# Mixture-of-experts tail of a four-batch attention kernel: 15 whole tiles at the end, or 16 steps of two half tiles in two runs that begin while the last batch is still being routed

## What is computed

```python
x = x + L0_xattn(layernorm(x), ctx, mask0)          # 2 heads of 64, context 512
x = x + L0_ffn(layernorm(x))                        # sigmoid(xr@Wr) * (relu(xk@Wk)**2 @ Wv), xk/xr mix a token with the one before it
x = x + L1_xattn(layernorm(x), ctx, ctx, mask1)     # 16 heads of 8, context 512
h = layernorm(x)
e = argmax(h @ router.T)                            # 8 experts, one for each token
x = x + down[e] @ (silu(gate[e] @ h) * (up[e] @ h)) # gate, up: 352x128; down: 128x352
```

## Time and profile before

| | us |
|---|---|
| median of 3 runs | 301.01 |
| lowest and highest | 298.39, 303.46 |
| the profiled execution, its own time | 302.52 |
| its span, first to last instruction | 300.7 |
| mean granted clock of TensorE | 0.92 of full |

### The profile page before, as it was taken

One profiled execution on the slowest core, in us unless ns is written; L12 is line 12 of the kernel. 1 busy time (PEld: TensorE's weight loads), 2 busy tenths in 40 slices (PEclk: granted clock), 3 DMA queues, 4 the chain that ended last, 5 costly groups with the idle time before them and its releaser, 6 DMA issues.

```text
span 300.7 us, 5435 instructions
## 1 busy us (share of the span) xinstructions
PE 254.9 (85%) x1878; PEld 135.1 (45%) x1878; DVE 186.5 (62%) x637; ACT 142.5 (47%) x268; POOL 75.3 (25%) x90
## 2 busy tenths in 40 slices
PE   0799998695898999999999999999998421999993
PEld 0345666464453244444434343343434220477872
DVE  3280966869877676778768868678643251244551
ACT  1167464433044366546666655656666100244540
POOL 2643592605203400003110203002031211023443
PEclk9999999899596699999999999999999855599997
DMA  6990366240646349998001940042000003601000
GB/s 180 401 416 11 99 152 157 59 134 25 148 117 163 101 149 275 289 256 259 13 2 34 291 203 2 0 147 83 2 0 2 35 0 109 192 8 33 18 16 2
DMA packets 19083, 34.46 MB, mean 115 GB/s; under 512 B 1407, under 2 KB 16386, under 8 KB 18096
## 3 DMA queue, kind: packets, MB, share of 16 engines
q1 hardware_dynamic: 9408, 23.58, 25.6%
q10 hardware_dynamic: 8784, 8.95, 11.3%
q0 software_dynamic: 864, 1.58, 1.6%
HBM read 21.74 MB, written 12.82 MB: 115 GB/s over the span
## 4 chain that ended last, share of the span: by engine, by line
PE 48%; DVE 9%; ACT 6%; issue 3%; DMA 2%; POOL 1%; POOLq 0%; DVEq 0%; SPq 0%; ACTq 0%
PE banks L1186 9%; PE banks L1172 8%; PE banks L1102 7%; PE banks L1167 5%; DVE scores_unused L839 5%; PE banks L1241 4%; PE banks L1242 3%; ACT p_region L626 3%; PE banks L1263 3%; PE banks L971 2%; ACT q_region L610 2%; PE banks L1255 2%; PE banks L977 1%; DMA binned_dram<-token_rows,mask_bias 1%; PE banks L1072 1%
## 5 line engine op out<-in xcount | busy, mean ns | idle before, releaser
L839 DVE CUSTOM_DVE_ANT_0 scores_unused<-banks,mask_bias 128x512 bf16<-128x512 f32 x128 | 82.8, 688 | 22.8 <-PE banks L1102 22.0
L626 ACT ACTIVATE p_region<-banks 128x1024 f32<-128x1024 f32 x64 | 65.3, 1022 | 57.4 <-PE banks L1172 57.2
L1102 PE MATMUL banks<-k_region,q_region 80*128 80x512 bf16 x128 | 41.9, 401 | 2.1 <-DVE max L839 1.7
L426 POOL TENSOR_TENSOR ln_rstd<-ln_var_eps,minus_half 128x2 f32<-128x2 f32 x16 | 12.2, 764 | 123.6 <-DVE ln_var_eps L692 123.6
L1172 PE MATMUL banks<-q_region,k_region 80*128 80x256 bf16 x256 | 40.3, 282 | 0.0
L1186 PE MATMUL banks<-p_region,values 128*9 128x256 f32 x512 | 34.3, 388 | 1.0 <-ACT p_region L626 1.0
L1172 PEld LDWEIGHTS banks<-q_region,k_region 80*128 80x128 bf16 x256 | 20.2, 99 | 16.8 <-issue 15.0
L1167 PE MATMUL banks<-mask_bias_by_key,ident_bf 64*64 64x512 bf16 x256 | 26.8, 408 | 0.6 <-ACT q_region L610 0.6
L515 POOL DMA_INDIRECT out_dram<-q_region x15 | 14.7, 979 | 34.0 <-DVE q_region L960 33.0
L950 DVE SCALAR_TENSOR_TENSOR q_region<-q_region,banks 128x352 f32<-128x352 f32 x15 | 7.8, 522 | 24.0 <-ACT q_region L655 24.0
L509 POOL DMA_INDIRECT binned_dram<-token_rows,mask_bias x8 | 8.3, 1038 | 55.4 <-DVE mask_bias L822 54.1
(11 more groups left out here) (146 smaller groups left out, 399.5 us busy)
## 6 DMA issues: line engine op xcount, KB each, us to landing
binned_dram<-ctx_region ACTq DMA_DIRECT2D x1, 8224.0 KB, 37.0
k_region<-k_parts_dram SPq DMA_DIRECT2D x4, 1152.0 KB
k_region<-gate_up_dram SPq DMA_DIRECT2D x1, 2816.0 KB, 13.2
q_region<-q_parts_dram SPq DMA_DIRECT2D x12, 192.0 KB
k_region<-mask1k_dram SPq DMA_DIRECT2D x1, 2048.0 KB, 12.0
k_region<-mask_dram SPq DMA_DIRECT2D x1, 2048.0 KB, 16.4
q_region<-binned_dram SPq DMA_DIRECT2D x15, 128.5 KB, 2.7
k_parts_dram<-q_region SPq DMA_DIRECT2D x4, 384.0 KB, 2.8
```

Of the source, the lines that this page charges most:

```text
L626: a.activation(pt[:, u % 2, j, :, :].rearrange("p (c t) q -> p c (t q)", c=2), ps[:, c:c + 2, :], ACT.Exp, scale=float(D1) ** -0.5).then_i ...
L839: return v.tensor_tensor_reduce(out=junk[:, q, :], in0=scores, in1=m1b[:, QT * (u // 4) + q, :], scale=1.0, scalar=-3e38, op0=ALU.add, op1 ...
L1102: return m.matmul(out, qst[0:R, (u * GH + j) * SQ + q * P:(u * GH + j) * SQ + (q + 1) * P], kst[0:R, (u * GH + j) * SK:(u * GH + j + 1) * ...
```

## The change

1. **Two runs.** Batches 0 to 2 (768 tokens) and batch 3 (256 tokens) have bins and tables of their own. The first run has 10 steps, the second 6: 16 in one pipeline.
2. **Half tiles.** A step still takes 128 rows, but as two halves of 64, each with its own expert and place (20 and 12 halves are enough for any split). Every product with expert weights is issued twice, once for each half, to PSUM partitions 0 to 63 and 64 to 127.
3. **Weights of the second half.** The first half reads its expert in the resident weights `moe_w` at a register's address. The second half's expert (1088 floats on 128 partitions, 557 KB) is copied from DRAM for each step by SyncE into a ring `stage` of seven places. The rows of a step come with two DMAs of 64 rows.
4. **Registers.** TensorE loads the one register it needs at the start of each step (`load_expert`), 16 times, in place of 15 at once. SyncE loads its own in seven loads.
5. **Batch 3 between the steps.** `BEHIND` is gone; `BESIDE2` puts `oT` to `pos`, `cnt` and `tab` (the table) of batch 3 between the parts of steps -1 to 4. Batch 2's chain moves up by a slot or so, and `cnt` and `tab` of the first run stand at (14, 3) and (15, 0).

```diff
-SLOT_TILES = (TOK - E) // P + E
+HALF = P // 2
+PHASE_BATCHES = (range(B - 1), range(B - 1, B))
+PHASE_TOK = tuple(SQ * len(bs) for bs in PHASE_BATCHES)
+PHASE_STEPS = tuple((E + (n - E) // HALF + 1) // 2 for n in PHASE_TOK)
+PHASE_AT = (0, PHASE_STEPS[0])
+STEPS = sum(PHASE_STEPS)
...
+EXPERT = 2 * I + 3 * D
+STAGES = 7
+STAGES_SOONER = 3
...
-    (13, 1): [("oT", 2)], (13, 2): [("wO", 2)], (14, 0): [("s4", 2)], (14, 1): [("n4", 2)], (14, 2): [("nT", 2)],
-    (14, 3): [("lg", 2), ("hot", 2)], (15, 1): [("pos", 2)],
+    (13, 1): [("oT", 2)], (13, 2): [("wO", 2)], (13, 3): [("s4", 2)], (14, 0): [("n4", 2)], (14, 1): [("nT", 2)],
+    (14, 2): [("lg", 2), ("hot", 2)], (14, 3): [("cnt", 0)], (15, 0): [("pos", 2), ("tab", 0)],
 }
-BEHIND = [(name, B - 1) for name in ("oT", "wO", "s4", "n4", "nT", "lg", "hot", "pos")] + [("cnt", 0)]
+BESIDE2 = {(-1, 1): [("oT", 3)], (0, 0): [("wO", 3), ("s4", 3)], (1, 0): [("n4", 3)], (1, 1): [("nT", 3)], (2, 0): [("lg", 3)],
+           (2, 1): [("hot", 3)], (3, 1): [("pos", 3), ("cnt", 1)], (4, 1): [("tab", 1)]}
...
+            def weights_in(s):
+
+                if s >= STAGES:
+                    sp.wait_ge(y_ready, s - STAGES + 1)
+                sp.dma_start(stage[:, s % STAGES, :], moe_d[:, bass.ds(second[s] * EXPERT, EXPERT)]).then_inc(staged[s % STAGES], 16)
...
             sp.wait_ge(experts_done, 1)
...
+            where(0, range(0, 2))
+            whose(0, range(0, STAGES_SOONER))
+            for s in range(STAGES_SOONER):
+                weights_in(s)
+            sp.wait_ge(scattered, 16 * QT * len(PHASE_BATCHES[0]))
+            for s in range(0, 2):
+                rows_in(0, s)
+            where(0, range(2, PHASE_STEPS[0]))
+            for s in range(2, PHASE_STEPS[0]):
+                rows_in(0, s)
+            whose(0, range(STAGES_SOONER, PHASE_STEPS[0]))
+            sp.wait_ge(st_ready, UNITS * GH)
+            for s in range(STAGES_SOONER, PHASE_STEPS[0]):
+                weights_in(s)
+            sp.wait_ge(experts_done, 2)
+            first = PHASE_AT[1]
+            where(1, range(first, first + 2))
+            whose(1, range(first, first + 2))
             sp.wait_ge(scattered, 16 * TILES)
...
-            pe.wait_ge(experts_done, 1)
-            _, expert = nc.values_load_multi_w_load_instructions(experts, engines=[pe.engine], min_val=0, max_val=E - 1,
...
+            def load_expert(s):
...
+                pe.wait_ge(experts_done, ph + 1)
+                n = s - PHASE_AT[ph]
+                _, r = nc.values_load_multi_w_load_instructions(experts[ph][:, n:n + 1], engines=[pe.engine], min_val=0, max_val=E - 1,
...
+            def half_weights(s, r, c, n):
+
+                if r == 0:
+                    return moe_w[:, bass.ds(expert[s] * EXPERT + c, n)]
+                return stage[:, s % STAGES, c:c + n]
...
                 if there(s + 1):
-                    e = expert[s + 1]
+                    load_expert(s + 1)
                     pe.wait_ge(gT_copied, s + 2)
+                    pe.wait_ge(staged[(s + 1) % STAGES], 16 * ((s + 1) // STAGES + 1))
                     if s >= 1:
                         pe.wait_ge(h_done, s)
-                    m.matmul(ps[:, 2 + 2 * nxt, 0:I], ginT[:, nxt, :], gu[:, bass.ds(e * (2 * I), I)], start=True, stop=True)
-                    m.matmul(ps[:, 3 + 2 * nxt, 0:I], ginT[:, nxt, :], gu[:, bass.ds(e * (2 * I) + I, I)], start=True, stop=True)\
-                        .then_inc(gu_ready, 1)
+                    for k in range(2):
+                        first, second = (half_weights(s + 1, r, k * I, I) for r in range(2))
+                        m.matmul(ps[0:HALF, 2 + k + 2 * nxt, 0:I], ginT[:, nxt, 0:HALF], first, start=True, stop=True)
+                        last = m.matmul(ps[HALF:P, 2 + k + 2 * nxt, 0:I], ginT[:, nxt, HALF:P], second, start=True, stop=True)
+                    last.then_inc(gu_ready, 1)
...
-                    for n, (c, rows) in enumerate(ITILES):
-                        last = m.matmul(ps[:, 6, 0:P], hT[0:rows, nxt, n * P:(n + 1) * P], dn[0:rows, n, bass.ds(e * D, D)],
-                                        start=n == 0, stop=n == 2)
+                    for n, (_, rows) in enumerate(ITILES):
+                        first, second = (half_weights(s - 1, r, 2 * I + n * D, D) for r in range(2))
+                        c = n * P + HALF
+                        m.matmul(ps[0:HALF, 6, 0:P], hT[0:rows, nxt, c - HALF:c], first[0:rows], start=n == 0, stop=n == 2)
+                        last = m.matmul(ps[HALF:P, 6, 0:P], hT[0:rows, nxt, c:c + HALF], second[0:rows], start=n == 0, stop=n == 2)
```

More of the change, by code:

```diff
@@ L329, in pipeline @@
         def pipeline(step):
-            for s in range(-2, SLOT_TILES + 1):
-                step(s, s % 2, lambda n: 0 <= n < SLOT_TILES)
+            for s in range(-2, STEPS + 1):
+                step(s, s % 2, lambda n: 0 <= n < STEPS)
         @block.sync
@@ L411, in _, with where @@
-            sp.wait_ge(scattered, 16 * TILES)
-            for s in range(SLOT_TILES):
-                sp.dma_start(gin[:, s, :], bins_d[bass.ds(at[s] * P, P), :]).then_inc(gin_in[s], 16)
+            sp.dma_start(moe_w[:, 7 * EXPERT:], moe_d[:, 7 * EXPERT:]).then_inc(moe_w_in, 16)
+            at, second = {}, {}
+            def where(ph, steps):
+                n = len(steps)
+                lo = 2 * (steps[0] - PHASE_AT[ph])
+                _, r = nc.values_load_multi_w_load_instructions(row_halves[ph][:, lo:lo + 2 * n], engines=[sp.engine], min_val=0,
+                                                                max_val=E * BIN_HALVES[ph] - 1,
+                                                                skip_runtime_bounds_check_because="the table is clamped to it")
+                for k, s in enumerate(steps):
+                    at[s] = r[2 * k:2 * k + 2]
@@ new lines, in whose @@
+            def whose(ph, steps):
+                lo = PHASE_STEPS[ph] + steps[0] - PHASE_AT[ph]
+                _, r = nc.values_load_multi_w_load_instructions(experts[ph][:, lo:lo + len(steps)], engines=[sp.engine], min_val=0,
+                                                                max_val=E - 1,
+                                                                skip_runtime_bounds_check_because="the table is clamped to it")
+                for k, s in enumerate(steps):
+                    second[s] = r[k]
@@ new lines, in _ @@
+            for s in range(STAGES_SOONER, PHASE_STEPS[0]):
[4 more added lines that the diff above has]
+            whose(1, range(first, first + 2))
+            sp.wait_ge(scattered, 16 * TILES)
+            for s in range(first, first + 2):
+                rows_in(1, s)
+                weights_in(s)
+            where(1, range(first + 2, STEPS))
+            for s in range(first + 2, STEPS):
+                rows_in(1, s)
@@ L414, in _ @@
+            whose(1, range(first + 2, STEPS))
+            for s in range(first + 2, STEPS):
+                weights_in(s)
             for r in range(YBUFS):
-                sp.wait_ge(out_done[r], 16 * len(range(r, SLOT_TILES, YBUFS)))
+                sp.wait_ge(out_done[r], 16 * len(range(r, STEPS, YBUFS)))
         @block.gpsimd
@@ L499, in _, with scatter @@
             output_bias(3)
-            pool.wait_ge(ids_set, 1)
-            for b in range(B):
-                inverse_root("s4", b)
-                if b == 0:
-                    pool.wait_ge(bins_blank, 16)
+            def scatter(b):
                 pool.wait_ge(ln4_done, b + 1)
@@ L643, in _ @@
             copy_out(UNITS - 1)
-            for kind, b in BEHIND:
-                beside(kind, b)
-            act.wait_ge(slot_done, B)
             def step(s, par, there):
@@ L660, in step @@
                     a.activation(ginT[:, par, :], ps[:, 0, 0:P], ACT.Copy).then_inc(gT_copied, 1)
+                for kind, b in BESIDE2.get((s, 0), []):
+                    beside(kind, b)
                 if there(s):
@@ L668, in step @@
                     last.then_inc(hT_copied, 1)
+                for kind, b in BESIDE2.get((s, 1), []):
+                    beside(kind, b)
             pipeline(step)
@@ L793, in beside @@
                     places(b)
+                if kind == "cnt":
+                    halves_of_experts(b)
+                if kind == "tab":
+                    table(b)
             def per_tile(c, b):
```

182 lines of the change are left out of this document (111 added, 71 removed).

## The result

| | before | after |
|---|---|---|
| median, same series (us) | 301.35 (4 runs) | 322.67 (4 runs) |
| lowest and highest | 298.39, 303.46 | 317.98, 325.88 |
| profiled execution: time, span | 302.52, 300.7 | 325.88, 324.0 |
| its mean granted clock | 0.92 | 0.908 |
| start of the last unit's transposes (`oT`) | 235.50 | 250.60 |

The ratio is 1.066 (95% interval 1.043 to 1.088). The forecast was 302, with 293 to 317 as its range: too low by some 21 us, outside the range, and a slower kernel where "within 2%" was the likeliest.

A forecast was written before the change was run, and what follows sets the result against it. TensorE's 18.4 us pause after the attention and its 2.29 us steps bound the kernel. 14.6 us won at the start, less 4.0 (ramp), 2.3 (extra step), 7.4 (12 steps), 2.0 (batch 3, tail): 302, range 293 to 317.

The forecast's parts named there:

- Costs at nothing: ScalarE ... stay below TensorE: In the expert steps, ScalarE's 1.13 us and GpSimd's 0.87 us a step stay below TensorE's step and cost nothing.
- The floor by the weights of gate 3: Gate 3's weights, issued behind 20 row loads and two register loads, land at 252.4; it doesn't decide gate 3 at 254.5.
- the ramp: From the first row transpose at 239.7 to gate 3 at 254.5: 10.8 us as now plus 4.0 us, at the lower clock.
- Its last weights ... land by 281, before gate 13: Batch 3's last weights, six copies with eight row loads behind the first four, land by 281, before gate 13.
- The clock back at 1.2 GHz in the pauses of the steps: TensorE's clock falls in pauses between steps, making it slow; 0.03 chance, together with weights or rows later than their cover.
- the term that decides: TensorE's one-register load each step, between down and gate: 0.5 us long, adding 0.38 us a step, ends 0 and 1.87.
- the halves run beside each other: In gate, up and down, both half products overlap: no doubling counted, 0 for down, which was the less sure.
- The changes of shape: Each step goes from full-width transposes to half products and back: 2 x 0.12 = 0.24 us a step.
- the load is hidden: Rival: the register load costs nothing, the step is 2.53 us and the time 296.3; chance 0.28.
- The staged weights bind: Rival: steps wait for their 557 KB at 218 GB/s and rows, some 3.0 us a step, 303, inside the forecast.
- The load stalls: Rival: the register load between down and gate stalls TensorE a microsecond or more a step, 312 to 322; chance 0.24.
- the halves of down don't overlap: Rival: the two half products of down run one after the other, 13 x 0.64 = 8 us, 310; chance 0.05.

## Why the prediction was wrong, point by point

1. **The step that failed: "Costs at nothing: ScalarE ... stay below TensorE".** It counted ScalarE's work in the steps and never the fills. The fill's line is in the functions that the diff touches, one DMA of 8224 KB had become two, and no price was asked for the second; not even the text on the change named it. The attention's end came 15.1 us late, of the 22.3 us by which the span missed (324.0 against 301.7), and the experiments put 13.4 to 15.3 us to the second fill; without it the ratio is 1.031.
2. **The floor by the weights of gate 3, mis-sized.** The step took 20 row loads at 0.57 us each and two long register loads, with the copy landed at 252.4, 16.9 us after `oT`. The 20 row loads took 15.18 us with a register load of 0.99 among them, 0.71 us each without it; the two register loads, 0.99 and 1.48, are the 2.5 that was put down for them. The weights landed 20.0 us after `oT`. So they decided, where the text says that the floor "doesn't decide". Gate 3 came only 1.0 us later than forecast, because the ramp itself, forecast at 19.0 us, takes 16.2 when nothing waits: two errors that nearly cancel.
3. **"Its last weights ... land by 281, before gate 13".** It should have been asked of gate 12, and the chain of waits ahead of it was shorter on paper. Batch 3's scatter started at 282.0, 31.4 us after `oT` (25.5 forecast), SyncE's first row load of that run followed at 287.36, and the weights, behind eight row loads at 0.78, were there only at 302.9. The hole and its slow clock cost 6.5 us: 3.46 + 2.56 + 0.50 above 2.58 at gates 12 to 14.
4. **The clock after the holes.** The prediction had TensorE at full clock from gate 3. After the hole before it, steps 3 to 5 take 5.89, 4.69 and 2.80 us, 5.6 above three of 2.58, of which I had allowed 1.5 for batch 3's work. With rows and weights in turn, where no hole stands ahead of them, the same three steps take 9.6 us, 1.9 above; so some 3.7 of the 5.6 go with the hole. "The clock back at 1.2 GHz in the pauses of the steps" was given 3% together with all late rows and weights. The windows show 0.68 for 268 to 284 us and 1.00 for 284 to 299:

```profile
268.00:284.00 16.00, 12.52 (x82) 7.31 (x84) 5.97 (x25) 3.65 (x15) 3.71 (x4) 0.68 0.69 253
284.00:299.00 15.00, 15.00 (x141) 8.80 (x138) 8.58 (x26) 6.77 (x29) 6.93 (x8) 1.00 0.50 156
```

5. **The register load, called the term that decides, is nothing.** It was put at L = 0.5 us with a lead of 0.27. The loads of one register, in the view of their line,

```profile
L1343 PEldq TENSOR_LOAD <-mask_bias x16: 298/302/492, 256.0 to 312.3; - x16
```

take 0.30, and the sequencer's lead is more like 0.9. With rows and weights in turn a load is at

```profile
L1341 PEldq TENSOR_LOAD <-mask_bias x1: 306/306/306, 261.8 to 261.8; - x1
```

and the gate product behind it, in the timeline of the same kernel, at

```profile
262.67 0.46 PE L1362 MATMUL banks<-k_region,q_region 128*64 x1
```

The 0.27 had been read from an address computation that stands right before its product, which is the least lead and not the usual one. Two loads a step changed nothing in most steps. The floor of some 600 ns that the Trainium skill gives for a register load ("DMA: Bandwidth & Descriptors", "Latency and other measured facts") does not hold here: 0.30 us was measured for one value. The other figure that the prediction set against the trace, 200 ns for each register, gives by its own formula 0.2 - 0.27 + 0.15 = 0.08 us, nearly but not quite hidden; and all register loads here read a tile in SBUF, so that they say nothing of loads from elsewhere.
6. **Right:** the halves run beside each other, down products too. L1364 and L1365 start 0.01 us apart, four pairs take 1.18 us (0.59 + 0.59 in the earlier trace rows) and six down pairs 0.81, 0.14 more than 0.67. The changes of shape, forecast at 0.24 us a step, are 0.18 to 0.29. The step is 2.58 and not 2.91, so 12 steps gave back 4.0 us that the forecast had spent. The tail behind the last gate is 10.3 us, 10.8 forecast.

The sum behind `oT`: 1.0 (gate 3) + 6.5 (hole at gate 12) + 5.6 - 1.5 (steps 3 to 5) - 4.0 (12 steps) - 0.5 (tail) is 7.1 us above the forecast; the traces say 7.2 (73.4 against 301.7 - 235.5 = 66.2).

Of the rivals, *the load is hidden* was true of the load, and its 296.3 is near what the kernel does once the fill and SyncE's order are out of the way (297.68). *The staged weights bind* named the right part and the wrong mechanism: not the rate of the copies, which keep pace with 2.58 us steps when they are issued in turn, but their place behind rows that are wanted later. *The load stalls* and *the halves of down don't overlap* are refuted. The rival that came about, an engine of the attention held by its own DMA issue, was in no list.

Not settled: why the second issue is held (the runs show when and how long), the 0.11 us between gates and row transpose, the clock of the first 100 us, and how short the ramp can get.

## What to carry to other kernels

Go through a diff by every DMA that it splits, and ask which engine issues the second one and whether the first is still being written then: the cost is the issuing engine's, and all that waits for it. Where rows and weights share an issuing queue, write out its order with 0.6 to 0.8 us for each issue and set each landing against the step that wants it; issue them in the order of the steps. A pause is priced with the slow clock behind it, here 3.5 us of waiting and 3 more of slow steps.

## What was not expected of the hardware

A DMA issue that takes 0.4 us by itself held its engine for 2.0, 8.9 and 15.5 to 16.0 us behind an unfinished transfer of 2048, 4096 and 6144 rows of 1028 bytes on the same queue, while a single transfer of 8192 such rows held it for 0.41. Two products on the two column halves of TensorE start 0.01 us apart and take the time of one. A register load of one value takes 0.30 us on TensorE's sequencer (0.49 at most), and two a step disappear in most steps. The time of a load isn't a plain count of its values. SyncE's eight loads in the changed kernel (the text on the change says seven), those of rows' places and those of experts,

```profile
L434 SPq TENSOR_LOAD <-mask_bias x4: 303/622/993, 246.2 to 291.1; - x4
L443 SPq TENSOR_LOAD <-mask_bias x4: 298/582/1479, 246.9 to 298.1; - x4
```

take 0.30 us for four values (at 286.4 and at 298.1), but 0.72 for the first four (at 246.2), 0.47 for two, 0.99 for sixteen and 1.48 for seven, beside 1.74 for fifteen in the kernel before. What makes them differ wasn't tried.
